# Layer 2 of a four-layer kernel: the next sequence's entry and gates placed in the output stage, attention outputs divided in place of the gates, value experts laid out with the expert innermost

## The reference, cut to what matters

```python
gates = sigmoid(x @ w_gate)                       # per token, head, expert
gm = one_hot(argmax(gates)) * gates               # one expert per token and head
values = einsum('bhne,ehdk,bnd->bhnk', gm, value_experts, x)
attn = softmax(causal(q @ k.T * SCALE))
out = einsum('bhij,bhjk->bhik', attn, values)
out = einsum('bhne,ehkd,bhnk->bhnd', gm, output_experts, out).sum(heads)   # then residual
```

## Time and profile before

| | |
|---|---|
| time, median of 3 runs | 3698.51 us (3696.15 to 3699.43) |
| the profiled execution | 3697.23 us, its span 3695.5 us |
| mean granted clock of TensorE | 0.942 of 2.4 GHz |
| busy: PE, DVE, ACT, POOL | 3274.7, 1997.1, 1494.3, 771.8 us |
| layer 2, four sequences | 342 to 2098 us of the span |

### The profile page before, as it was taken

The page is one execution under the profiler, slowest core; times in us unless marked ns, Lnnn a source line. Parts: engine busy times, 40 slices in busy tenths (PEclk is TensorE's granted clock), DMA queues, the critical chain, the costliest instruction groups (busy, mean ns, idle before and its releaser), DMA issues. The chain is left out here.

```text
span 3695.5 us, 50581 instructions
## 1 busy us (share of the span) xinstructions
PE 3274.7 (89%) x18322; PEld 2349.5 (64%) x18322; DVE 1997.1 (54%) x3358; ACT 1494.3 (40%) x2706; POOL 771.8 (21%) x724
## 2 busy tenths in 40 slices
PE   7896989889889888889898699898998979999998
PEld 4554745876459754687457664645556458888887
DVE  4345844668446764459545565674756643333333
ACT  2321144421444134441344247465564634444443
POOL 1121500653007420265004410101001011111111
PEclk9897999999999999999999899999999989999999
DMA  5102100201011100111002101000010040000000
GB/s 183 48 34 70 46 1 1 78 32 39 1 31 47 47 23 1 51 40 35 23 1 70 66 1 13 13 2 24 2 23 3 2 167 12 12 12 17 7 7 12
DMA packets 175604, 119.82 MB, mean 32 GB/s; under 512 B 116609, under 2 KB 157825, under 8 KB 171905
## 3 DMA queue, kind: packets, MB, share of 16 engines
q1 hardware_dynamic: 175360, 116.54, 10.7%
HBM read 99.18 MB, written 28.31 MB: 34 GB/s over the span
## 5 line engine op out<-in xcount | busy, mean ns | idle before, releaser
L874 POOL TENSOR_TENSOR l2c_rlo<-l2c_routed,l2c_rhi 128x512 fp32r<-128x512 f32 x256 | 347.1, 1369 | 914.5 <-ACT l2c_rhi L900 875.6
L1410 ACT ACTIVATE l3b_prob<-sums 128x512 f32<-128x512 f32 (+3 forms) x768 | 333.3, 493 | 203.7 <-PE sums L1343 164.6
L1659 PE MATMUL sums<-l_uhi,l_h 128*128 128x512 f32 x1024 | 405.8, 396 | 0.0
L1659 PE MATMUL sums<-l_ulo,l_h 128*128 128x512 f32 x1024 | 405.6, 396 | 0.0
L806 DVE TENSOR_REDUCE l2b_mx<-sums 128x1 fp32r<-128x1024 f32 (+7 forms) x256 | 193.0, 757 | 315.7 <-PE sums L687 313.8
L713 PE MATMUL sums<-l2b_prob,l_vx 128*128 128x512 f32 (+3 forms) x768 | 309.3, 513 | 38.6 <-DVE l_oT L798 23.8
L743 ACT ACTIVATE l2b_prob<-sums 128x512 f32<-128x512 f32 (+3 forms) x384 | 181.2, 489 | 316.2 <-PE sums L704 311.5
L984 PE MATMUL sums<-l2c_ohi,l2c_rhi 128*128 128x256 f32 x1024 | 295.8, 289 | 12.7 <-POOL l2c_rlo L874 11.8
L984 PE MATMUL sums<-l2c_ohi,l2c_rlo 128*128 128x256 f32 x1024 | 293.4, 287 | 0.0
L984 PE MATMUL sums<-l2c_olo,l2c_rhi 128*128 128x256 f32 x1024 | 293.3, 286 | 0.0
L1338 PE MATMUL sums<-l_qst,l_kst 64*128 64x512 f32 (+3 forms) x768 | 279.0, 428 | 14.9 <-ACT l3b_prob L1410 6.4
(11 more groups left out here) (259 smaller groups left out, 7513.6 us busy)
## 6 DMA issues: line engine op xcount, KB each, us to landing
l_ve<-ve SPq DMA_DIRECT2D x34, 512.0 KB, 3.8
l_oe<-oe SPq DMA_DIRECT2D x16, 1024.0 KB, 6.0
l2c_word<-weights_copy SPq DMA_DIRECT2D x32, 352.0 KB, 3.9
sb_nx<-sums SPq DMA_DIRECT2D x10, 1024.0 KB, 5.6
weights_copy<-h SPq DMA_DIRECT2D x2, 4096.0 KB, 25.7
l_qst<-l3b_peak SPq DMA_DIRECT2D x512, 0.5 KB, 2.0
l_h<-weights_copy SPq DMA_DIRECT2D x2, 4096.0 KB, 23.5
sb_nx<-tokens SPq DMA_DIRECT2D x5, 1024.0 KB, 5.3
```

Source lines behind the costliest of these rows:

```text
L874: pool.tensor_tensor(rlo[:, i % RT, :], routed[:, i % RT, :], rhi[:, i % RT, :].bitcast(F32), ALU.subtract).then_inc(s.routed_lo, 1)
L1410: act.activation(prob[:, i % RB, j, a, 0:hi - lo], bank(m.ps, part % SCORE, 0, hi - lo), ACT.Exp, scale=SCALE1).then_inc(s.exp_ready, 1)
L1659: run(lambda out, a, x, first, last: pe.matmul(out, a, x, start=first, stop=last))
```

## The change

Entry and gates: a block ahead of the loop turns the first sequence's tokens and makes its gates. In the loop, the output stage does this for the next sequence: DVE's statistics at block 1, the scale from block 6, PE's transposes every third block from 10 through one bank (7), the logits at 35, DVE's gate steps one a block from 37. The masks have three banks. The value stage begins with the splits; xhi is made by ACT. The last pass does the entry once more, unused. The unnormalised gates are split and turned at the start of attention. At the end of each head ACT copies the outputs, DVE writes the reciprocals of the 64 denominator rows, and POOL, which is otherwise idle there, multiplies. The DMAs of the denominators and the work on normalised gates are gone. The value experts' columns are ordered (k, e) in place of (e, k).

```diff
+    def entry_turn(pe, t):
+        if t:
+            pe.wait_ge(s4.xT_ready, t)
+        for c in range(KC):
+            last = pe.transpose(bank(m.ps, ENTRY, c * P, (c + 1) * P), m.nx[:, t, c * P:(c + 1) * P], m.ident[:, :])
+        last.then_inc(s4.transposed, 1)
+
+    def entry_take(act, t):
+        act.wait_ge(s4.transposed, t + 1)
+        act.copy(xT[:, :, t * P:(t + 1) * P], bank(m.ps, ENTRY, 0, D).rearrange("p (c q) -> p c q", c=KC)).then_inc(s4.xT_ready, 1)
...
+        return [clamped, lambda: None, raised,
+                lambda: step(dve.reciprocal(g[:, :], z[:, :])),
+                lambda: step(dve.tensor_reduce(top[:, :], by_head(g), AX_X, ALU.max)),
+                lambda: step(dve.tensor_tensor(by_head(first), by_head(g), every(top), ALU.is_equal)),
+                lambda: step(dve.tensor_tensor(by_head(first), by_head(first),
+                                               prio[:, :].unsqueeze(1).to_broadcast([P, NT * H0, NE]), ALU.mult)),
+                lambda: step(dve.tensor_reduce(win[:, :], by_head(first), AX_X, ALU.max)),
+                lambda: step(dve.tensor_tensor(by_head(first), by_head(first), every(win), ALU.is_equal)),
+                lambda: dve.tensor_tensor(gm[:, :], first[:, :], g[:, :], ALU.mult).then_inc(s4.gm_ready, 1)]
...
+                    act.copy(xhi[:, :, cols], xT[:, :, cols]).then_inc(s.x_hi, 1)
...
-                    dve.tensor_tensor(vm[:, n % VM, :].rearrange("p (e k) -> p e k", e=NE),
-                                      bank(m.ps, n % RING).rearrange("p (e k) -> p e k", e=NE),
-                                      gm[:, at:at + NE].unsqueeze(2).to_broadcast([P, NE, DH0]), ALU.mult).then_inc(s.value_masked, 1)
+                    dve.tensor_tensor(by_key(vm[:, n % VM, :]), by_key(bank(m.ps, n % RING)),
+                                      gm[:, at:at + NE].unsqueeze(1).to_broadcast([P, DH0, NE]), ALU.mult).then_inc(s.value_masked, 1)
                     if not pooled(n):
                         dve.wait_ge(s.value_masked, n + 1)
-                        dve.tensor_reduce(vx[:, t, h, vcol(h)], vm[:, n % VM, :].rearrange("p (e k) -> p k e", e=NE),
-                                          AX_X, ALU.add).then_inc(s.v_ready, 1)
+                        dve.tensor_reduce(vx[:, t, h, vcol(h)], by_key(vm[:, n % VM, :]), AX_X, ALU.add).then_inc(s.v_ready, 1)
...
-                        slot = vm[:, n % VM, :]
-                        step(pool.tensor_tensor(slot[:, 0:256], slot[:, 0:256], slot[:, 256:512], ALU.add))
-                        step(pool.tensor_tensor(slot[:, 0:128], slot[:, 0:128], slot[:, 128:256], ALU.add))
-                        pool.tensor_tensor(vx[:, t, h, vcol(h)], slot[:, 0:64], slot[:, 64:128], ALU.add).then_inc(s.pool_v_ready, 1)
+                        slot = by_key(vm[:, n % VM, :])
+                        step(pool.tensor_tensor(slot[:, :, 0:4], slot[:, :, 0:4], slot[:, :, 4:8], ALU.add))
+                        step(pool.tensor_tensor(slot[:, :, 0:2], slot[:, :, 0:2], slot[:, :, 2:4], ALU.add))
+                        pool.tensor_tensor(vx[:, t, h, vcol(h)], slot[:, :, 0], slot[:, :, 1], ALU.add).then_inc(s.pool_v_ready, 1)
...
-                def den_row_out(h):
-                    sp.wait_ge(s.den_read, h + 1)
-                    sp.dma_start(dens[h:h + 1, :], den[den_row(h), h % 2, :]).then_inc((s.even_den_out, s.odd_den_out)[h % 2], 16)
...
+                def turn_gates():
+                    pe.wait_ge(s.hilo_ready, 1)
+                    for t in range(NT):
+                        last = pe.transpose(bank(m.ps, 3 + t // 4, (t % 4) * P, (t % 4 + 1) * P),
+                                            hilo[:, t, :, :].rearrange("p a b -> p (a b)"), m.ident[:, :])
+                        if t % 4 == 3:
+                            last.then_inc(s.gates_turned, 1)
...
+                    if h == k == 0:
+                        pe.wait_ge(s.gmT_ready, NH)
...
-                            warm(pe, 6, 8)
+                            turn_gates()
+                            warm(pe, 6, 4)
...
-                def den_out(h):
+                def head_out(h):
                     act.wait_ge(s.pv_mm, NT * (h + 1))
                     if h >= 2:
-                        act.wait_ge((s.even_den_out, s.odd_den_out)[h % 2], 16 * (h // 2))
-                    act.copy(den[den_row(h), h % 2, :], bank(m.ps, PV, 0, T, den_row(h))).then_inc(s.den_read, 1)
+                        act.wait_ge(s.o_ready, h - 1)
+                    act.copy(oT[vcol(h), h // 2, :], bank(m.ps, PV, 0, T, vcol(h))).then_inc(s.o_read, 1)
...
-                        den_out(h2 - 1)
-                    if (h2, k2) == (H0 - 1, 3):
-                        fetch_sd(act, m, s)
-                den_out(H0 - 1)
+                        head_out(h2 - 1)
+                    if x == 3:
+                        for n in range(NH):
+                            act.wait_ge(s.gates_turned, n + 1)
+                            act.copy(gmT[:, n * HALF:(n + 1) * HALF], bank(m.ps, 3 + n)).then_inc(s.gmT_ready, 1)
...
-                def head_out(h):
+                def den_out(h):
                     dve.wait_ge(s.pv_mm, NT * (h + 1))
-                    dve.tensor_copy(oT[vcol(h), h // 2, :], bank(m.ps, PV, 0, T, vcol(h))).then_inc(s.o_read, 1)
-
+                    if h >= 2:
+                        dve.wait_ge(s.o_ready, h - 1)
+                    dve.reciprocal(rden[vcol(h), h % 2, :], bank(m.ps, PV, 0, T, dens(h))).then_inc(s.den_read, 1)
+
+                tiles = lambda x: x.rearrange("p (t n) -> p t n", t=NT)
+                dve.tensor_copy(gates_hi, gm[:, :]).then_inc(s.gates_hi, 1)
+                dve.wait_ge(s.gates_hi, 1)
+                dve.tensor_copy(hilo[:, :, 0, :], tiles(gates_hi.bitcast(F32)))
+                dve.tensor_tensor(hilo[:, :, 1, :], tiles(gm[:, :]), tiles(gates_hi.bitcast(F32)),
+                                  ALU.subtract).then_inc(s.hilo_ready, 1)
...
-                fetch_stats(dve, m, s)
-                fetch_norm(dve, m, s)
-                head_out(H0 - 1)
+                        den_out(h2 - 1)
...
+                for h in range(H0):
+                    pool.wait_ge(s.o_read, h + 1)
+                    pool.wait_ge(s.den_read, h + 1)
+                    part = oT[vcol(h), h // 2, :]
+                    pool.tensor_tensor(part, part, rden[vcol(h), h % 2, :], ALU.mult).then_inc(s.o_ready, 1)
...
+        MASKS = 3
+        turn_at = {10 + 3 * t: t for t in range(NT)}
+        LOGITS_AT, GATES_FROM, EXP_AT, SD_AT, NORM_FROM = 35, 37, 38, 5, 6
...
+                    if i == SD_AT:
+                        fetch_sd(act, m, sf)
+                    if i in turn_at:
+                        entry_take(act, turn_at[i])
+                    if i == EXP_AT:
+                        gate_exp(act)
...
+                    if i == 1:
+                        fetch_stats(dve, m, sf)
+                    if i == NORM_FROM:
+                        fetch_rstd(dve, m, sf)
+                    if NORM_FROM < i <= NORM_FROM + NT:
+                        fetch_scale(dve, m, sf, i - NORM_FROM - 1)
+                    if 0 <= i - GATES_FROM < len(gates):
+                        gates[i - GATES_FROM]()
...
-                dve.wait_ge(s.out_mm, len(blocks))
                 for t in range(NT):
+                    dve.wait_ge(s.out_mm, len(blocks) - (t < NT // 2))
                     dve.tensor_tensor(m.x[:, t, :], m.x[:, t, :], m.ps[:, t * D:(t + 1) * D], ALU.add).then_inc(s.y_ready, 1)
...
-                        if i >= 4:
-                            pe.wait_ge(s.routed, i - 3)
-                        pe.matmul(bank(m.ps, 4 + i % 4), sel[:, c * NE + e, :], gmT[:, n * HALF:(n + 1) * HALF],
+                        if i >= MASKS:
+                            pe.wait_ge(s.routed, i - MASKS + 1)
+                        pe.matmul(bank(m.ps, 4 + i % MASKS), sel[:, c * NE + e, :], gmT[:, n * HALF:(n + 1) * HALF],
...
+                    if i in turn_at:
+                        pe.wait_ge(sf.nx_ready, turn_at[i] + 1)
+                        entry_turn(pe, turn_at[i])
+                    if i == LOGITS_AT:
+                        gate_logits(pe)
...
-    ve = i["L0_ffn_value_experts"].transpose(2, 1, 0, 3)
+    ve = i["L0_ffn_value_experts"].transpose(2, 1, 3, 0)
```

147 lines of the change are left out of this document (66 added, 81 removed).

## The result

The changed kernel takes 3923.81 us (median of four runs, 3910.67 to 3931.28), the kernel before 3698.42 beside it: a ratio of 1.0606, with an interval of 1.0576 to 1.0637, so slower by 225 us. The prediction said 3932 and slower. The profiled execution has a span of 3918.6 us, 223.1 more than before.

What follows compares the result with a forecast made beforehand. PE sets the pace, and whatever lengthens DVE's read of the PV banks at head boundaries delays it. 149+58-2-31-3+42+21 (the last the prologue) = +234 us on 3697.2 gave 3931, to the median 3932; range 3860 to 3985.

Steps and rivals of the forecast that it cites:

- The reciprocal's price: Head boundaries: DVE's reciprocal of 64x1024 takes 6.55 us, on a line through the 64- and 512-column rows.
- rival (c): Head boundaries: the reciprocal costs more per column, up to 8.9 us; 66 us more, 3998 in all; chance 0.05.
- (d): Head boundaries: the reciprocal runs at the copy's rate, so boundaries cost as today; 3725 us; chance 0.02.
- The boundaries and the clock: Head boundaries: 28 waits longer by 5.33 us, +149; low clock afterwards, 2.5 us at 23 of them, +58.
- The 6 us for the sqrt: Last head of attention: the next entry's sqrt with two table loads leaves ACT, -1.5 us each, -6 in all.
- Rival (b): Head boundaries: PE's clock stays up behind the gaps, so the +58 us falls away; 3874 us; chance 0.10.
- End of attention: Last head to first output product: old and new chains come out alike, -0.5 us a sequence, -2 in all.
- Start of attention: Gate transposes replace warming matmuls and DVE's first reduction moves by 0.8 us: +3; with the sqrt's -6, -3.
- Value stage: Start -2 us, PE's wait for the gates with its low clock -18, DVE's lag at the end -11: -31.
- what is left ahead of the first value matmul is the table load: Start of value stage: table load, experts' rounding and POOL's subtraction remain once entry leaves; after PE's cold start, -2 us.
- Output stage: Entry's PE work +28 us, PE stalls of 5 near block 40 +20, final sums one block earlier -6: +42.
- statistics and scaling early on stay in the cover: Early output stage: DVE's entry work fits in the 1.9 us before PE needs its products, adding no stall.

Runs made afterwards that it cites:

- experiment 1: The changed kernel with the reciprocal at each head's end replaced by a plain copy of the same 64x1024 sums; 3706.13 us, ratio 1.0036.
- experiment 5: The kernel before with only the value experts' columns reordered, expert innermost; 3672.53 us, ratio 0.9949.
- experiment 9: The changed kernel with the output stage's eight scalings of the next entry replaced by statistics instructions over the same tiles; 3920.24 us, ratio 1.0610.
- experiment 8: The changed kernel with the entry's scaling, transposes and gate steps placed later in the output stage, gates' reciprocal in four pieces; 3902.80 us, ratio 1.0555.

## Why the prediction held, and which of its terms were off

**The reciprocal's price** came out to the digit: 6.555 us against 6.55. Two widths from the trace of before, on one line, were enough; rival (c) is out, and so is (d): a copy of the shape takes 1.222. The estimate from the Trainium skill (VectorE: DVE Perf Modes, First, the fixed hardware budget), 8.5 us, is out as well: the measurement decides.

**The boundaries and the clock.** 149+58 = 207 us were predicted for the head boundaries; the heads grew by 196.6, and 197.1 against experiment 1. The idle is as predicted: PE's waits ahead of the weighted sums went from 38.6 to 186.7, 148.1 more against 149. The clock term was mis-sized: with the same instructions PE's busy time in the heads went from 597.9 to 646.4 us, 48.5 more where the sum had 58, and 148.1+48.5 = 196.6. The sum took 2.5 us at 23 boundaries from one pair of rows; 48.5 over 23 are 2.1 each. The 6 us for the sqrt are not seen: with the copy of experiment 1 the heads are only 0.5 us shorter than before. Rival (b), the clock stays up, needed a window near 1.00 behind a gap; it reads 0.71.

**End of attention**: -1.2 against -2. Experiment 1 shows what is inside: without the division's length this piece would be 22.5 us shorter than before. The division on the rows does pay here (no denominators' DMA and transpose); the reciprocal of the last head, which nothing hides, takes 21.3 of it back.

**Start of attention**: -1.8 against +3. The layout alone gives 7.6 there, by less low clock (experiment 5), which the sum had not; against experiment 5 the piece is 5.8 longer, so the gates' transposes and copies cost about twice the 3 us.

**Value stage.** PE's wait for the gates is gone and the matmuls are 17.6 us shorter (predicted 18), the tail 10.0 (11). Experiment 5 splits this: the layout alone gives the tail and about 10 of the 17.6. The start was undersized: -16.0 us over three gaps against -8 with the final sums. The step that failed is "what is left ahead of the first value matmul is the table load": it is not left, the changed kernel has no table load in its value stage (why, no run shows). The timeline of the changed kernel:

```profile
857.98 1.04 ACT L584 CAST l2a_vhi<-l_ve 128x1024 fp32r<-128x1024 f32 x1 [12.10 <-issue]
859.10 2.34 POOL L620 TENSOR_TENSOR l2a_vlo<-l_ve,l2a_vhi 128x1024 fp32r<-128x1024 f32 x1 [11.85 <-ACT l2a_vhi L584]
859.36 8.58 DVE L598 TENSOR_TENSOR l2a_xlo<-l_xT,l2a_xhi 128x256 fp32r<-128x256 f32 x8 [7.65 <-ACT l2a_xhi L589]
861.78 0.80 PE L573 MATMUL sums<-l2a_vhi,l2a_xhi 128*128 128x512 f32 x1 [11.52 <-DVE l2a_xlo L598]
```

From ACT's first rounding to the first matmul it is 3.8 us; before, the table load of 1.28 stood ahead of ACT's copies, the logits of 3.68 on PE from 788.37 on the earlier trace rows, and the matmul came 7.6 us after the load's start. That is 3.8 us at each of three gaps, 11 of the 16.

**Output stage.** This term was mis-sized as much as the clock: +57.5 against +48 without the final sums. Its parts were off by more than its sum. PE's own work for the entry is some 21 us and not 28: the transposes add 0.2 us to a block, 1.7 a sequence, where the sum took 3.35 from a row at a lower clock and with waits between (the window 1222 to 1226 of the kernel before reads 0.63). The logits add 3.6. The stall near block 40 was there, DVE's reciprocal of 3.34 us from 1291.58, and PE:

```profile
1293.80 0.35 PE L1036 MATMUL sums<-l2c_ohi,l2c_rhi 128*128 128x256 f32 x1 [1.58 <-POOL l2c_rlo L933]
1296.49 0.49 PE L1026 MATMUL sums<-l_gmT,l_sel 128*128 128x512 f32 x1 [1.04 <-DVE l2c_routed L991]
1298.58 0.36 PE L1036 MATMUL sums<-l2c_ohi,l2c_rhi 128*128 128x256 f32 x1 [1.59 <-POOL l2c_rlo L933]
```

Blocks 36 to 47 take 27.0 us in place of 20.5, 6.5 more against the 5 predicted. The step that failed is "statistics and scaling early on stay in the cover": four blocks take 10.4 us in place of 7.1, in all four sequences but for one with 8.9. From 1224.9 to 1237 DVE has no idle (experiment 9's rows), the products of two neighbouring blocks start 4.5 us apart (1226.18 and 1230.68), where PE needs one each 1.68, and PE stands still:

```profile
1233.50 0.36 PE L1036 MATMUL sums<-l2c_ohi,l2c_rhi 128*128 128x256 f32 x1 [1.59 <-POOL l2c_rlo L933]
...
1233.00:1237.00 4.00, 3.50 (x20) 3.43 (x21) 4.00 (x7) 2.13 (x4) 3.37 (x4) 0.71 0.72 293
```

Each item had been costed against the cover by itself, and a check of the weights and an expert's subtraction that fall into the same blocks were not added. In this trace that is 12 of the stage's 57.5 us; 1.8 us a sequence are the stall, the rest is low clock, which not every sequence has (experiment 9). Beside POOL's subtractions the scalings take longer, but that is worth little to PE there. With three mask banks in place of four the mask products wait too once DVE is late, which the prediction had excluded: 13.9 us in their group, against none for DVE before.

```profile
L1026 PE MATMUL sums<-l_gmT,l_sel 128*128 128x512 f32 x256 | 111.5, 442 | 51.6 <-PEq L678 37.7 <-DVE l2c_routed L991 13.9
```

Whether a fourth bank would save any of it was not tried; the products behind them are late in the same places.

**Sum.** Against the prediction the heads came out 4.4 us lower (clock and idle 10.4 lower, the sqrt's 6 not gained), the start of attention 4.8 lower, the output stage 9.5 higher, the start of the value stages 8 lower, the prologue 2.5 lower, the others together 2.2 higher: 8 us under the 234, and 3 us more lie outside the pieces. So that the sum is so close is partly luck, by errors that cancel; the mechanism is not, nor the idle of 148 us that makes two thirds of the change.

## What to carry to other kernels

Where an engine must empty a buffer before PE may go on, the duration of that one instruction is paid at each hand-over, however idle the engine is on average: read first what PE waits for, copy it out, and do the long work (here the reciprocal) in pieces, from the copy, behind it. For the same reason look at what stands in the queue ahead of such a read: moving it in front of a split that nobody waited for took 29 us out of the heads, more than the new layout gave in all. And a gap of PE costs more than its length: price the low clock behind it too, from a row of the same kernel. Last, a piece of one trace is a number with a spread: the same output stage read 496.6 to 502.8 us in four kernels, so a gain of 4 us was found only by looking block by block, where it turned out to be mostly clock.

## What the runs showed of the hardware that was not expected

- How far DVE stands still beside POOL (experiment 9), at its most, at the start of the value stage: its first three subtractions of 128x256 take 6.90 us together, the next five about 0.41 each; all three overlap POOL's work from 859.10 on. The kernel before has the same (a rounding of 128x256 in 2.28 us, 0.286 elsewhere).
- POOL's three additions with operands 8 floats apart in the last one take 727, 399 and 308 ns in the changed kernel, against 737, 461 and 322 with the contiguous halves of before: no slower. DVE's reduction over strided input, in contrast, takes 1074 against 686.
- A reciprocal in four pieces of 128 columns costs 0.946 us each (experiment 8), 3.78 us in place of 3.34 as one: 0.15 us for each cut, which is what makes spreading it cheap.
